# Slot one-hots of a token router: scalar-operand instructions per token tile in place of broadcast ones

## The reference

```python
xn = (x - mu) * rsqrt(var + EPS) * gamma + beta
probs = softmax(einsum('btd,ed->bte', xn, router_w) / TEMP)
w, idx = top_k(probs, 2)                      # of E = 8 experts
wdense = sum(one_hot(idx, E) * w[..., None], axis=-2)
h = silu(einsum('btd,edf->betf', xn, W1))     # f = 512
out = einsum('bte,betd->btd', wdense, einsum('betf,efd->betd', h, W2)) + res
```

## Time and profile before

| what | us |
|---|---|
| median of 3 runs | 831.33 |
| the runs | 831.33, 836.5, 829.42 |
| the profiled execution, its own time | 832.6 |
| its span, first to last instruction | 830.5 |
| mean granted TensorE clock, share of full | 0.906 |
| TensorE busy | 653.1 (79%) |
| VectorE busy | 471.9 (57%) |
| GpSimd busy | 374.4 (45%) |
| ScalarE busy | 324.2 (39%) |

### The profile page before, as it was taken

One profiled execution on the slowest core, in us unless ns is written; L12 is line 12 of the kernel. 1 busy time (PEld: TensorE's weight loads), 2 busy tenths in 40 slices (PEclk: granted clock), 3 DMA queues, 4 the chain that ended last, 5 costly groups with the idle time before them and its releaser, 6 DMA issues.

```text
span 830.5 us, 29323 instructions
## 1 busy us (share of the span) xinstructions
PE 653.1 (79%) x11332; PEld 513.4 (62%) x11332; DVE 471.9 (57%) x1716; ACT 324.2 (39%) x536; POOL 374.4 (45%) x384
## 2 busy tenths in 40 slices
PE   4752877899978789898898988677658799888880
PEld 2421676798977546565665656455448688776760
DVE  7867787622235475665757665675876842123224
ACT  3450253232223226465655757366445222222220
POOL 4613583595776300222312100350177677777770
PEclk9865799999989959999999999999856999999995
DMA  7510022122323312021221201010002111224325
GB/s 208 132 38 17 17 55 71 49 68 70 87 73 94 115 34 66 26 78 41 65 63 35 81 16 57 2 42 17 6 20 80 43 52 53 53 79 116 103 63 155
DMA packets 61300, 52.71 MB, mean 63 GB/s; under 512 B 9745, under 2 KB 54674, under 8 KB 61162
## 3 DMA queue, kind: packets, MB, share of 16 engines
q1 hardware_dynamic: 52306, 32.67, 13.5%
q0 software_dynamic: 8864, 18.17, 8.3%
HBM read 30.88 MB, written 19.92 MB: 61 GB/s over the span
## 4 chain that ended last, share of the span: by engine, by line
PE 41%; DVE 24%; issue 13%; POOL 7%; DMA 5%; DVEq 4%; ACT 4%; SPq 0%; POOLq 0%; ACTq 0%
PE stbank L1223 9%; PE bank L1329 4%; POOL xg L507 4%; PE sbank L1287 3%; PE sbank L1282 3%; PE stbank L1313 3%; PE stbank L1213 2%; DVE mx L902 2%; DVE zr L611 2%; DVE xs L859 2%; POOL ytab L514 2%; DMA xg<-table,idx 2%; DVE st L582 2%; PE stbank L1215 2%; PE stbank L1214 2%
## 5 line engine op out<-in xcount | busy, mean ns | idle before, releaser
L1223 PE MATMUL stbank<-wdn,g 128*128 x1136 | 171.4, 296 | 43.1 <-DVE ysb L838 38.7
L507 POOL DMA_INDIRECT xg<-table,idx x142 | 140.5, 989 | 133.4 <-DVE sidx L828 72.3
L994 ACT ACTIVATE g<-stbank 128x512 f32<-128x512 f32 x142 | 84.7, 597 | 263.5 <-PE stbank L1215 263.1
L1223 PEld LDWEIGHTS stbank<-wdn,g 128*128 128x128 f32 x1136 | 145.1, 200 | 61.4 <-issue 52.4
L902 DVE TENSOR_REDUCE mx<-sbank 128x2 f32<-128x320 f32 (+1 forms) x256 | 116.6, 472 | 62.9 <-PE sbank L1287 57.4
L1047 ACT ACTIVATE pT<-stbank 128x1024 f32<-128x1024 f32 (+1 forms) x128 | 116.6, 916 | 71.2 <-PE stbank L1313 70.7
L838 DVE COPY ysb<-stbank 128x128 f32<-128x128 f32 x142 | 41.2, 290 | 172.2 <-PE stbank L1223 110.8
L527 POOL DMA_INDIRECT cg<-yslot,posi x64 | 61.2, 956 | 128.7 <-ACT pT L1047 112.6
L1213 PE MATMUL stbank<-xT,wup 128*128 128x128 f16 x568 | 116.5, 229 | 2.0 <-issue 1.9
L1215 PE MATMUL stbank<-xT,wup 128*128 128x128 f16 x568 | 116.8, 229 | 0.0
L1214 PE MATMUL stbank<-xT,wup 128*128 128x128 f16 x568 | 115.2, 226 | 0.0
(11 more groups left out here) (211 smaller groups left out, 1060.9 us busy)
## 6 DMA issues: line engine op xcount, KB each, us to landing
yslot<-ysb SPq DMA_DIRECT2D x71, 64.0 KB
table<-tb SPq DMA_DIRECT2D x16, 256.0 KB, 2.3
cg<-ytab SPq DMA_DIRECT2D x16, 256.0 KB, 3.6
qz<-dumps SPq DMA_DIRECT2D x96, 32.0 KB
kst<-dumps SPq DMA_DIRECT2D x96, 32.0 KB
xg<-table,idx POOLq DMA_INDIRECT x142
xs<-in_x SPq DMA_DIRECT2D x8, 256.0 KB, 4.9
qz<-in_w SPq DMA_DIRECT2D x1, 2048.0 KB, 10.1
```

What stands on the lines that cost most here:

```text
L507: g.indirect_dma_start(xg[:, i % G].rearrange("p a d -> p (a d)"), None, table if t >= FIRST else table[0:CHUNK, :], bass.IndirectOffsetOn ...
L994: a.activation(g32[:, i % 3, :], hbank[i % 2], ACT.Silu, scale=1.0 / WSCALE).then_inc(s_g32, 1)
L1223: ins = mm(ybank, g32[:, i % 3, P * f:P * f + P], w[:, 0, P * f:P * f + P], start=(f == 0), stop=(f == FC - 1))
```

## The change

Steps 12 to 15 of the router on VectorE are written anew. Before, one instruction covered four token tiles of one choice: the compared row was broadcast over the token tiles, and the slot numbers over the columns. Now every token tile and choice has two instructions of its own. The tile one-hot compares `tile16` with one scalar per partition and multiplies the outcome by a second scalar per partition, in a single instruction; the lane one-hot compares `lane16` with one scalar per partition. The drain between comparison and multiplication is gone. Per step, 6 instructions and a drain become 16 instructions; over the 16 steps 96 become 256. Data types, buffers, semaphores and what TensorE reads stay as they are.

```diff
@@ -780,15 +780,11 @@
                     ts = slice(TPB * (k - 12), TPB * (k - 12) + TPB)
                     cols = slice(0, KEPT) if c == 0 else slice(FIRST, TILES)
                     n = cols.stop - cols.start
-                    for i in range(2):
-                        v.tensor_tensor(oht[:, i, ts, 0:n], tile16[:, cols].unsqueeze(1).to_broadcast([P, TPB, n]),
-                                        tilf[:, i, ts].unsqueeze(2).to_broadcast([P, TPB, n]), ALU.is_equal)
-                    dve.drain()
-                    for i in range(2):
-                        v.tensor_tensor(oht[:, i, ts, 0:n], oht[:, i, ts, 0:n],
-                                        token_id[:, i, ts].unsqueeze(2).to_broadcast([P, TPB, n]), ALU.mult)
-                        ins = v.tensor_tensor(ohl_[:, i, ts, :], lane16[:].unsqueeze(1).to_broadcast([P, TPB, P]),
-                                              lanf[:, i, ts].unsqueeze(2).to_broadcast([P, TPB, P]), ALU.is_equal)
+                    for t in range(ts.start, ts.stop):
+                        for i in range(2):
+                            v.tensor_scalar(oht[:, i, t, 0:n], tile16[:, cols], tilf[:, i, t:t + 1], token_id[:, i, t:t + 1],
+                                            ALU.is_equal, ALU.mult)
+                            ins = v.tensor_scalar(ohl_[:, i, t, :], lane16[:], lanf[:, i, t:t + 1], None, ALU.is_equal)
                     ins.then_inc(s_oh, 1)
```

## The result

The changed kernel takes 841.68 us (median of 4 runs, 840.65 to 842.77), the kernel before 830.44 us (median of 4, 829.42 to 836.5). The ratio, taken over these runs, is 1.0103, with a 95% interval of 1.0064 to 1.0141: +8.6 us by the ratio, between +5.3 and +11.7. The medians differ by more, 11.2 us; the four runs of the kernel before scatter over 7 us. The prediction was 841.4.

The account below looks back on a forecast made before the run. No engine was taken as the limit throughout; VectorE's four one-hot passes were held to be on the path. +8.9 us for them and +1.2 for GpSimd's port gave +10.1 on 831.3: 841.4 us, range 836 to 849.

Parts of the forecast that it names:

- The pair's price: One `oht` plus one `ohl` instruction on VectorE: 0.202 + 0.165 = 0.367 us, against a break-even of 0.287 us.
- Pass 1: One-hots of chunk 0, first layer, with nothing beside them: 11.84 us against 9.48, +2.4 us.
- Passes 2 and 4: One-hots beside the first expert tiles in each layer, where VectorE sets the tile rate: +2.2 us each.
- Pass 3: One-hots of chunk 2 in the last attention batch, TensorE waiting: +2.4 us less 0.25 of slack, +2.1.
- GpSimd's port: Passes 2 and 4: GpSimd's indirect DMAs hold VectorE's one-hots, 0.1 us for each of 12, +1.2 us (0 to 2.5).
- The sum: Whole kernel: +8.9 us from the four passes and +1.2 from GpSimd's port, +10.1 us in total.
- Cheap scalar operands: Rival: scalar operands are read behind the preceding instruction's stream; pair 0.192 us, -8.2 us, 823 us; chance 0.03.
- One and two columns a cycle: Rivals: new one-hots stream slower than four columns a cycle; one: 849 us, chance 0.09; two: 847 us, chance 0.10.
- No difference: Rival: the second scalar operand is free, pair 0.308 us, near break-even; about +2 us, 833 us; chance 0.09.
- GpSimd holding VectorE: Rival: each of 12 indirect DMAs stops the one-hots some 0.6 us beyond the 0.1; +7, 848 us; chance 0.06.
- No make-up later: After the passes: the forecast is wrong if TensorE's tiles run closer together and make up the delay.

Follow-up runs that it names:

- f32_row: The changed kernel with the row that `ohl` is compared with (`lane16`) held in f32 instead of f16: 846.36 us, 16.5 above the kernel before.
- immediates: The changed kernel with scalars as instruction constants, not read from memory, in passes 1 and 2 only (result differs): 831.33 us, 1.5 above the kernel before.
- oht_only: The kernel before with only the tile one-hots (`oht`) made by two-scalar instructions, lane one-hots still broadcast: 838.48 us, 8.7 above the kernel before.
- ohl_only: The kernel before with only the lane one-hots (`ohl`) made by one-scalar instructions, tile one-hots still broadcast: 831.11 us, 1.3 above the kernel before.

## Why the prediction was right, point by point

- *The pair's price.* Forecast 0.202 + 0.165 = 0.367 us, measured 0.200 + 0.162 (starts in pass 1: 0.20 and 0.16). The duration of `ohl`, forecast as 0.25, is 0.24. Both parts of the price, scalars and stream, were measured apart and hold. One piece of its evidence was weaker than it looked: L768 (32 and 39 columns) lasts no longer than L732 (8 columns), but two columns a cycle should have added 12 to 16 ns too, so the row fits neither that rate nor one column a cycle. Only `f32_row` and `immediates` settled the rate.
- *Pass 1.* Forecast 11.84 us, measured 11.68.
- *Passes 2 and 4.* Forecast 2.95 us a step, measured 3.32 - 0.40 = 2.92, thus +2.1 and +2.0 us for the passes where +2.2 each was forecast.
- *Pass 3.* Forecast +2.1, measured +2.2 to the copy of the sums (5.98 less the 3.76 at the start of the pass). TensorE takes the last group 0.05 us after VectorE's end (602.47 after 602.42), where it came 0.25 later before: the slack was used up, as the step says. To the last index instruction it is +1.9, because both profiles of the kernel before show a pause of 0.43 us between two of the index instructions that the changed kernel does not have; its cause is open.
- *GpSimd's port.* This term was mis-sized: forecast +1.2 us, measured next to nothing. In the profile of the changed kernel one start in pass 2 came 0.06 us late and none in pass 4; on the slower chip two starts of pass 4 came late, by 0.09 and 0.05 us. The stretched instructions are there, at the ends of the indirect DMAs: `ohl` at 152.19 lasts 0.44 and ends at 152.63, while GpSimd ran

```profile
151.67 0.94 POOL L507 DMA_INDIRECT xg<-table,idx  x1 [1.61 <-PE sbank L1190]
```

  until 152.61. But the next instruction starts at 152.35, 0.16 us later as everywhere (rows of pass 2 above). What an indirect DMA holds is mostly the end of the instruction, and that costs time only where something waits for the end. L821 in the earlier trace rows was such a case, and it was misread as 0.21 us lost:

```profile
670.67 0.30 DVE L822 SCALAR_TENSOR_TENSOR key<-key,pad_row 128x46 f32<-128x46 f32 x1
671.05 0.19 DVE L825 TENSOR_SCALAR idx<-lg 128x46 uint32<-128x46 f32 x1
```

  L822 started on time, 0.10 us behind L821. Behind it stands a drain, and there 0.38 us passed to the next start where it is 0.28 undisturbed (the same two instructions of the changed kernel, 679.25 and 679.53): 0.10 us lost. The one-hots have no drain; the change took theirs away. The full lock-out of the Trainium skill ("SBUF — State Buffer", Who interferes with whom) is not what a chain of such instructions pays here beside an indirect DMA. Beside the tensor operation of GpSimd it is: behind L588 at 613.48 the next VectorE instruction started at 614.98, after 1.50 us.
- *The sum.* 8.9 + 1.2 = 10.1 was forecast for it, 8.3 is what the spans differ by, and 8.6 (5.3 to 11.7) what the timed ratio says. That the median of 841.68 lies so near the 841.4 is luck: the step was 1.5 to 1.8 us smaller than forecast, most of it the port's 1.2, and the scatter of the two medians, 11.2 us apart, made up for it.
- *The rivals.* Cheap scalar operands (pair 0.192) is about what `immediates` shows (0.18), with scalars that are not read from memory; so its arithmetic was sound and its condition false. One and two columns a cycle are excluded for `ohl` by the gap of 0.162 and by `f32_row`. No difference is excluded by the pair's 0.36 us against 0.308 and by `oht_only`. GpSimd holding VectorE for 0.6 us each time is excluded by the starts in passes 2 and 4.
- *No make-up later.* The delay after pass 4, 8.6 us, is 8.3 at the end. Between passes 2 and 3 it fell from 5.0 to 3.8, which the drift of such a stretch, up to 1.9 us, covers; whether a part was made up there can't be told.

By the formula of the Trainium skill ("VectorE: DVE Perf Modes", The TRN2 errata), which has no term for scalars, the pair would have been an estimated 0.165 us; `immediates` comes near it with 0.18, and the changed kernel with its scalars is at 0.36.

## What to carry to other kernels

Price an instruction by the gap to the next start, in three parts: base, scalars from memory, and columns at the rate of the types. One broadcast instruction over several tiles beats a row of scalar-operand ones unless each has many columns: here a fixed price of 0.13 us (one scalar) or 0.19 (two) stood against columns of 0.26 ns in place of 1.0. From the measured gaps I estimate where the two forms break even: near 145 columns for the one-hot with one scalar (0.129 us and 0.26 ns a column, against 0.150 us per token tile at 128 columns, less or more by 1.0 ns a column), and near 75 to 80 for the one with two, which also saves the multiplication (0.190 us and 0.26 ns a column, against 0.136 us at 40 columns and 2.0 ns for each more). If a broadcast comparison is the cost, make all its operands 16-bit and give it an innermost dimension in which no operand stands still (tried here only together); and read off which engine takes over (TensorE at 2.0 us a tile, GpSimd at 2.57) before counting on the gain.

## What the runs showed that I had not expected

- A VectorE instruction held by GpSimd's indirect DMA ends up to 0.20 us late (0.44 in place of 0.24 us), and the instruction behind it starts on time or at most 0.09 us late, in the two profiles of the changed kernel.
- The hold goes the other way too. The indirect DMA of pass 2 takes GpSimd 0.94 us in the changed kernel, but up to 1.44 in the kernel before. The broadcast lane one-hots have a part in it: the DMA takes up to 1.85 us in `oht_only`, which keeps them, and at most 0.98 in `ohl_only`, which doesn't. In each of these long cases such a comparison ran as the DMA began, and VectorE's two copies came behind it; which of the two holds GpSimd is not shown. GpSimd waits 1.3 us or more for TensorE ahead of these DMAs in the kernel before, so they cost nothing there. Timelines of GpSimd in pass 2 of the kernel before, `oht_only` and `ohl_only`:

```profile
150.98 1.44 POOL L507 DMA_INDIRECT xg<-table,idx  x1 [1.37 <-PE sbank L1194]
```

```profile
154.28 1.85 POOL L507 DMA_INDIRECT xg<-table,idx  x1 [1.36 <-PE sbank L1192]
```

```profile
153.61 0.94 POOL L507 DMA_INDIRECT xg<-table,idx  x1 [1.96 <-PE sbank L1195]
```

- Scalars from memory beside 2-byte data leave the rate at four columns a cycle: `ohl`'s gap is 0.162 us and grows by 0.033 with an f32 row. With two scalars the 40 columns are too few to tell.
- A broadcast operand does not stop two columns a cycle if it is f16 and moves over the innermost dimension, even over four elements only: 1024 columns in 0.60 us. Type and pattern were changed together; which of them alone would do was not tried.
- The same kernel before took 830, 834 and 886 us on three chips. On the slow one the changed kernel's pass 1 lasted 11.6 us, as on the fast one (11.7), and its pass 2 12.9 (13.0); the 52 us by which its profile is longer lie elsewhere, 24 of them between passes 2 and 3 and 26 behind pass 4, where expert tiles and attention run. What is slower there was not found.
